# Mixture-of-experts FFN on one core: the first picked row is weighed on ScalarE and added on GpSimd, the second stays on VectorE

## The reference

```python
def _L1_ffn_ref(x, gate_w, gate_b, sw1, sb1, sw2, sb2, rw1, rb1, rw2, rb2):
    hs = jnp.einsum('bsd,ndf->nbsf', x, sw1) + sb1[:, None, None, :]
    shared_out = jnp.einsum('nbsf,nfd->bsd', _swiglu(hs), sw2) + sb2.sum(0)
    probs = jax.nn.softmax(x @ gate_w + gate_b, axis=-1)
    topk_probs, topk_idx = jax.lax.top_k(probs, TOP_K)          # TOP_K = 2 of 8 experts
    cw = jnp.sum(jax.nn.one_hot(topk_idx, N_EXPERTS) * topk_probs[..., None], axis=2)
    hr = jnp.einsum('bsd,edf->ebsf', x, rw1) + rb1[:, None, None, :]
    out_e = jnp.einsum('ebsf,efd->ebsd', _swiglu(hr), rw2) + rb2[:, None, None, :]
    routed_out = jnp.einsum('ebsd,bse->bsd', out_e, cw)
    return shared_out + routed_out
...
x = x + 0.5 * _L1_ffn_ref(_layernorm(x, axis=-1), ...)
```

## Time and profile before

| | us |
|---|---|
| three timed runs: median (lowest to highest) | 2528.4 (2522.89 to 2532.07) |
| the profiled execution: its own time | 2514.7 |
| its span, first to last instruction | 2513.0 |
| busy in the span: PE / DVE / ACT / POOL | 2037.7 / 1847.8 / 887.5 / 888.2 |

### The profile page before, as it was taken

The page is one execution under the profiler, slowest core; times in us unless marked ns, Lnnn a source line. Parts: engine busy times, 40 slices in busy tenths (PEclk is TensorE's granted clock), DMA queues, the critical chain, the costliest instruction groups (busy, mean ns, idle before and its releaser), DMA issues. The chain is left out here.

```text
span 2513.0 us, 39639 instructions
## 1 busy us (share of the span) xinstructions
PE 2037.7 (81%) x11491; PEld 1345.7 (54%) x11492; DVE 1847.8 (74%) x3714; ACT 887.5 (35%) x1742; POOL 888.2 (35%) x891
## 2 busy tenths in 40 slices
PE   1599997789999738889858599999999864788985
PEld 1366666656666627677646233333333454566764
DVE  5688884478997766667978677777777277566696
ACT  1222223322221323333337255555555422233331
POOL 1344442144443556666325300000000136566641
PEclk9999996889999559999989699999999875899997
DMA  4000000100000522223325534444332033222234
GB/s 164 1 1 0 0 0 20 32 1 1 0 0 0 180 72 81 79 79 97 113 59 160 101 45 64 64 64 62 46 54 33 1 108 129 68 80 79 82 120 142
DMA packets 110259, 156.00 MB, mean 62 GB/s; under 512 B 20758, under 2 KB 77372, under 8 KB 109628
## 3 DMA queue, kind: packets, MB, share of 16 engines
q1 hardware_dynamic: 90416, 104.43, 18.1%
q0 software_dynamic: 17472, 48.80, 6.0%
q10 hardware_dynamic: 2252, 1.29, 0.2%
HBM read 107.00 MB, written 47.20 MB: 61 GB/s over the span
## 5 line engine op out<-in xcount | busy, mean ns | idle before, releaser
L1899 DVE TENSOR_REDUCE t_nm<-ps 128x1 f32<-128x512 f32 (+3 forms) x768 | 390.6, 552 | 105.8 <-PE ps L1989 52.9
L1965 ACT ACTIVATE t_E<-ps 128x1024 f32<-128x1024 f32 (+3 forms) x384 | 295.3, 809 | 247.5 <-PE ps L2017 194.3
L1377 PE MATMUL ps<-m_w,m_xT 128*128 (+1 forms) x1248 | 348.0, 414 | 0.0
L1377 PEld LDWEIGHTS ps<-m_w,m_xT 128*128 128x128 f32 x1248 | 223.3, 190 | 55.4 <-issue 4.5
L535 PE MATMUL ps<-wgT,f_xT 128*128 128x352 f32 x512 | 183.1, 505 | 37.4 <-DVE f_h L437 35.4
L496 POOL TENSOR_TENSOR f_h<-f_h,f_hmagic 128x704 f32<-128x704 f32 x64 | 108.1, 1689 | 291.8 <-DVE f_h L182 291.8
L2014 PE MATMUL ps<-t_Qs,t_Ks 98*128 98x512 bf16 (+3 forms) x768 | 200.6, 342 | 4.4 <-DMA t_Qs<-t_mT 3.3
L1397 PE MATMUL ps<-m_w,m_hT 128*128 (+1 forms) x1248 | 200.8, 297 | 1.3 <-DVE m_hT L1476 1.3
L569 PE MATMUL ps<-wdT,f_hT 128*128 128x256 f32 (+1 forms) x768 | 193.0, 394 | 7.4 <-DVE X L472 5.4
L1884 POOL COPY t_Va<-t_V 128x128 f32<-128x128 f32 x64 | 16.1, 296 | 494.2 <-DVE t_mp L1910 493.9
L1464 DVE TENSOR_TENSOR m_ab<-ps,m_b 128x512 f32<-128x512 f32 x208 | 143.3, 689 | 58.2 <-issue 47.2
(11 more groups left out here) (285 smaller groups left out, 4060.1 us busy)
## 6 DMA issues: line engine op xcount, KB each, us to landing
m_yl<-m_picked_out SPq DMA_DIRECT2D x64, 256.0 KB, 2.8
m_raw<-in_L_ffn_rw SPq DMA_DIRECT2D x48, 256.0 KB, 3.2
t_parts<-t_qkv_part SPq DMA_DIRECT2D x64, 192.0 KB, 2.9
t_Qs<-t_parts SPq DMA_DIRECT2D x96, 128.0 KB, 4.1
t_Ks<-t_parts SPq DMA_DIRECT2D x96, 128.0 KB, 6.7
m_rows<-m_xn SPq DMA_DIRECT2D x16, 512.0 KB, 4.2
m_xg<-m_rows POOLq DMA_DIRECT2D x64, 128.0 KB, 3.0
X<-in_L_attn_x SPq DMA_DIRECT2D x4, 1024.0 KB, 13.3
```

The costliest lines, as they stand in the source:

```text
L1377: last = nc.tensor.matmul(ps[:, H1 + u, :], xT[:, u, kx, k, :], of_expert(w1, kw, e, k), start=n == 0, stop=n == 3 * DC - 1)
L1899: nc.vector.tensor_reduce(dst, ps[:, bank, 0:n], AX_X, ALU.max, negate=True).then_inc(emptied, 1)
L1965: nc.scalar.activation(E[:, s % NPB, :, 0:n], ps[:, bank:bank + 2, 0:n], ACT.Exp, scale=float(HD) ** -0.5).then_inc(e_ok, 1)
```

## The change

Of the two picked rows of a tile, the first goes another way. ScalarE multiplies it in place by its weight (`weigh_first`, from step 76 on, tile s-76, behind `x_hi`); it now waits for the load. GpSimd adds it into X (`add_first`, also from step 76 on, behind the issue of the step's rows); it waits for ScalarE's `weighed` and for VectorE's `result` of that tile, and has a semaphore instruction (`fence`) between the waits and the add. VectorE keeps the second row, waits for `first_in` in place of the load, and has no drains. ScalarE's steps of the shared part are written out where a loop was. In the profile of the changed kernel the lines above 890 are moved on.

```diff
-    AT_ADD = 5
+    AT_SCALE, AT_ADD = 4, 5
...
+                def add_first(n):
+                    pool.wait_ge(weighed, n + 1)
+                    pool.wait_ge(y_ok, NT + n + 1)
+                    pool.sem_inc(ch.fence, 1)
+                    nc.gpsimd.tensor_tensor(ch.tile(n), ch.tile(n), yl[:, n % YL, 0, :], ALU.add).then_inc(first_in, 1)
...
                     if 2 <= s < NT + 2:
                         scatter(s - 2)
+                    if s - NT - AT_SCALE >= 0:
+                        add_first(s - NT - AT_SCALE)
+                for n in range(NS - NT - AT_SCALE, TILES):
+                    add_first(n)
...
-                steps(act, step)
+
+                def weigh_first(n):
+                    act.wait_ge(yl_in[n % YL], 16 * (n // YL + 1))
+                    nc.scalar.activation(yl[:, n % YL, 0, :], yl[:, n % YL, 0, :], ACT.Copy, scale=topw[:, 0, n:n + 1]
+                                         ).then_inc(weighed, 1)
+
+                for s in range(-2, RING):
+                    step(0, s, False)
+                with act.Fori(1, NT // RING - 1) as t:
+                    for c in range(RING):
+                        step(t, c, False)
+                for s in range(NT - RING, NS + 2):
+                    step(0, s, s >= NT)
+                    if s - NT - AT_SCALE >= 0:
+                        weigh_first(s - NT - AT_SCALE)
+                for n in range(NS + 2 - NT - AT_SCALE, TILES):
+                    weigh_first(n)
...
                 def add_picked(n):
-                    dve.wait_ge(yl_in[n % YL], 16 * (n // YL + 1))
-                    for k in range(2):
-                        x = ch.tile(n)
-                        nc.vector.drain()
-                        last = nc.vector.scalar_tensor_tensor(out=x, in0=yl[:, n % YL, k, :], scalar=topw[:, k, n:n + 1],
-                                                              in1=x, op0=ALU.mult, op1=ALU.add)
-                    last.then_inc(summed, 1)
+                    dve.wait_ge(first_in, n + 1)
+                    x = ch.tile(n)
+                    nc.vector.scalar_tensor_tensor(out=x, in0=yl[:, n % YL, 1, :], scalar=topw[:, 1, n:n + 1],
+                                                   in1=x, op0=ALU.mult, op1=ALU.add).then_inc(summed, 1)
```

More of the change, by code:

```diff
@@ L1257, in expert_ffn @@
         half_b2 = ch.sb(name + "half_b2", [P, D], ctx=ctx)
+        weighed, first_in = sem("weighed"), sem("first_in")
         turned, high, x_ok, h1_ok, ab_ok, silu_ok, h_ok, h_turned, h_high, hT_ok, out_ok, y_ok, biased, summed = map(
```

## The result

| | before | after |
|---|---|---|
| median of six runs, us | 2525.28 | 2508.26 |
| lowest to highest | 2515.04 to 2532.07 | 2499.65 to 2517.19 |
| the profiled execution: span | 2513.0 | 2497.9 |

The ratio of after to before is **0.9941**, with a 95% interval of 0.9914 to 0.9967 (the quotient of the two medians, 0.9933, lies inside it): the change makes the kernel 0.6% faster, some 15 us. The forecast was 2535 us and no change that can be measured. So it was wrong, and in the sign of the sum too: +6.2 us were worked out.

What follows compares the result with a forecast made beforehand. VectorE was taken to set the pace. Per pass +4.1 (steps 77 to 99), -1.4 (last four steps) and +0.4 (tail) make +3.1 us, +6.2 in two: 2535 us median, no measurable change; range 2498 to 2546.

Steps and rivals of the forecast that it cites:

- What bounds the kernel: Steps 77 to the last add: VectorE sets the pace; its list after the change would be 2.6 us a step.
- Where the new adds lie: Counted from B, a step's bias start: weighing 0.48 us, GpSimd's first add at B+1.98, VectorE's at B+2.2, so GpSimd first.
- It keeps VectorE out for two adds, 1.42 us: Steps 77 to 99: GpSimd's two adds hold VectorE's add to B+3.40; a step becomes 3.62 us, against 3.34.
- rival 2: VectorE let in between GpSimd's adds, its add ending 0.3 us after the first; 2.94 us steps, 2503 us; chance 0.10.
- the 23 steps: Steps 77 to 99, at 3.62 us each 83.3 us a pass, against 79.2 before.
- the one row of three adds: Step 97 before the change: three GpSimd bias adds in a row, VectorE's gate beside them 1.91 us, elsewhere 0.45.
- The last four steps: Steps 100 to 103, with one GpSimd add each: together 11.2 us, before 12.6, so -1.4 a pass.
- The tail: From the last step to the last add: 7.5 us, before 7.3; with GpSimd's last adds in VectorE's way, +0.4.
- ScalarE's unrolled loop: nothing: Writing out ScalarE's shared steps adds nothing to the time, as ScalarE has 70 us free of 99.

Runs made afterwards that it cites:

- experiment 7: Four variants of the kernel before: semaphore between GpSimd's last bias adds, gate as another operation, waits between adds, one wait ahead; gate 1.91 us, still held, 0.56, 0.61.
- experiment 4: The changed kernel with ScalarE's weighing put ahead of x_hi instead of behind it; ratio to the kernel before 0.9898.
- experiments 1 and 3: 1: the changed kernel with the last six tiles' picked rows added by VectorE alone, 0.9897; 3: that plus VectorE's add right behind the gate, 0.9826.
- experiment 6: Kernel before with VectorE's picked adds behind the gate, 1.0006; changed kernel with ScalarE weighing but VectorE making both adds, 1.0019.

## Why the prediction was wrong

By its own steps:

- **What bounds the kernel** held. The stretches are where the change acts, and VectorE's list there can go to 2.57 us, as worked out (2.6), once nothing holds it.
- **Where the new adds lie** held nearly to the digit: the weighing takes 0.50 us (0.48 was taken), GpSimd's first add starts at B+2.01 (B+1.98), VectorE's add at B+2.17 (B+2.2).
- **"It keeps VectorE out for two adds, 1.42 us": this step failed.** VectorE is out for one, to B+2.74, and the step is 2.94 instead of 3.62 us; its add ends 0.28 us behind GpSimd's first, which the prediction had named as the sign of rival 2. Over the 23 steps that is 67.85 us (1177.43 to 1245.28) where 83.3 were summed and rival 2 said 67.6. The step rested on the one row of three adds. That row was of another kind: it began directly behind a DMA issue, and the new pair doesn't (experiment 7). Where the pair does begin so, in step 77 of experiment 4, the 3.62 us are there (3.63): the size was right for that kind of row, and the prediction never asked of which kind its pair would be. The same trace had a case of the nearer kind, GpSimd's row of eleven, which has no issue ahead of it. I had used it for its hand-over only, and hadn't looked at VectorE's instructions beside it, with both inputs in SBUF and each GpSimd add 14.26 / 11 = 1.3 us long:

```profile
879.21 1.25 DVE L1039 TENSOR_TENSOR m_pr<-m_pr,m_small 128x256 f32<-128x256 f32 x1
...
881.86 1.24 DVE L1045 TENSOR_TENSOR m_pr<-m_pr,m_small 128x256 f32<-128x256 f32 x1
...
883.67 0.83 DVE L1008 TENSOR_TENSOR m_pr<-m_pr,m_small 128x256 f32<-128x256 f32 x1
884.58 1.33 DVE L1010 TENSOR_TENSOR m_pr<-m_pr,rank 128x256 f32<-128x256 f32 x1
```

  Had VectorE been kept out to the end of that row at 887.03, the first of these would have taken 7.8 us. It was let in after one add. Rival 2 had 0.10 and should have been the forecast. The Trainium skill's page "SBUF — State Buffer", section "Who interferes with whom", says that the lock is held for the whole instruction and that the order of issue decides. The 138 rows of experiment 7 agree with a lock per instruction. The 1.91 us of step 97 aren't explained by it unless the three adds count as issued together.
- **The last four steps** held: 11.24 us (1245.28 to 1256.52) for 11.2. **The tail** did too, 7.54 for 7.5, but the sum stopped at the last add. That GpSimd, idle at the end before, now works until VectorE's last add starts, and has its drain behind that, isn't in the prediction: +9.5 us in two passes, shown by experiments 1 and 3. It is a missing term; the forecast's 2535 would have been 2544 with it, so it doesn't excuse the forecast. Rival 2's 2503 would have become 2513, or 2510 from the later median of before (2525.28 for 2528.4); 2508.26 was measured. That this is so close is partly luck: in the profiled spans the routed parts took 7.1 us more and what lies ahead of the experts 6.0 us less, and neither is in any of the sums. The stated range held the time because rival 2 lay in it; the forecast itself was 27 us off.
- **"ScalarE's unrolled loop: nothing"** isn't settled. The first 68 steps of the routed part take 220.8 and 221.0 us before. After, they take 223.4 in m0, of which one interval of 5.36 us for 3.4 makes 1.9; one of 4.8 to 5.5 us also turns up in five of the eight kernels without GpSimd's new add, so it needn't be the change's. In m1 they take 225.9, of which some 3 us are the turn of the loop, every fourth step. The first row is before, the second after:

```profile
2255.55 0.69 DVE L1464 TENSOR_TENSOR m_ab<-ps,m_b 128x512 f32<-128x512 f32 x1 [0.67 <-issue]
```

```profile
2259.90 0.69 DVE L1491 TENSOR_TENSOR m_ab<-ps,m_b 128x512 f32<-128x512 f32 x1 [0.89 <-issue]
```

  To tell whether it is ScalarE's code, the kernel before ran with ScalarE's steps written out:

```diff
-                steps(act, step)
+                for s in range(-2, RING):
+                    step(0, s, False)
+                with act.Fori(1, NT // RING - 1) as t:
+                    for c in range(RING):
+                        step(t, c, False)
+                for s in range(NT - RING, NS + 2):
+                    step(0, s, s >= NT)
```

> The kernel before with ScalarE's shared steps written out instead of in a loop, as the changed kernel has them; nothing is weighed there, and the adds are those of before. In the kernels with the changed kernel's code the first 68 steps of the second pass take 223.2 to 225.9 us, with every fourth step (the turn of the loop) 3.60 or 3.75 us long, against 221.0 us and 3.54 us in all with the code of before. Theory A (the written-out steps on ScalarE make the loop's turn slower, by where the code lies or how it is fetched): this kernel too shows 223 us or more in its second pass. Theory B (what does it lies elsewhere, on GpSimd or VectorE, where the changed kernel has its new adds): 221.0 us.

  In its second pass the turn of the loop takes 3.5 us as before, and of the 223.7 us one interval of 5.48 makes 2. So ScalarE's code by itself doesn't do it. Four steps, one turn of the loop, take 13.2 us in m1 of all eight kernels without GpSimd's new adds, the one of experiment 6 with ScalarE's weighing among them. They take 13.4 in m1 of four of the six kernels with the adds and 13.3 in the two that have six of them fewer (experiments 1 and 3). So it comes with GpSimd's new adds or with what they changed on VectorE; by what path is open.

## What to carry to other kernels

When work moves to an idle engine, ask two things of the trace beside its busy time: when does it now finish last (its drain at the end of a block may no longer be hidden; here 4.8 us a pass, bought back by ending its share six tiles early), and which of the old engine's instructions it now holds up (here those of VectorE with both inputs in SBUF). Then order the old engine's list so that these stand together and the new engine's fall beside the rest: the same change gave 0.6% as it was made and 1.7% with these two edits. And before a stall is scaled up from one row, look for every row of its kind in the trace and ask how each began: here rows that start right behind a DMA issue hold VectorE to their end, and the others for one instruction.

## What the runs showed that I had not expected

- GpSimd's drain at a block's end finishes 5.32 us after the end of its last add, in all fourteen kernels and both passes: 1253.12 to 1258.4 before, 1263.54 to 1268.9 after, 1246.42 to 1251.7 with both edits. VectorE's takes 0.52 us.
- A row of GpSimd adds that starts 0.02 us or less behind a DMA issue keeps VectorE's instructions with two SBUF inputs out to its end (1.91 us through three adds, 1.52 through two). The same row started 0.09 us behind the issue gives way after one (0.61 us), and so does the one with waits between its adds (0.56 us).
